# One memory plan for four chained stages: the first loads, roundings, norms and transposes of a stage are issued inside the stage before it

## The reference, cut to what matters

```python
x = x + tanh(g_xattn[0]) * _L0_xattn_ref(_layernorm(x), ctx, ctx, Wq, Wk, Wv, Wo, bo, g)
x = x + tanh(g_ffn[0])   * _L0_ffn_ref(_layernorm(x), Wb, bias, Wr, A, Bm)
x = x + tanh(g_xattn[1]) * _L1_xattn_ref(_layernorm(x), ctx, ctx, mask, Wq, Wk, Wv, Wo)
x = x + tanh(g_ffn[1])   * _L1_ffn_ref(_layernorm(x), weight, bias, gate_w, in_scale, out_scale)

# _L0_xattn_ref: linear attention, 8 heads of 64
qh = softmax(qh, axis=-2) * SCALE; kh = softmax(kh, axis=-1)
context = einsum('bhdn,bhen->bhde', kh, vh)
out = einsum('bhde,bhdn->bhen', context, qh)        # then Wo, bo and an L2 norm
# _L0_ffn_ref: x @ Wb.T + bias, plus a rank-16 mixture of 8 experts, top 2
# _L1_xattn_ref: 32 query heads on 8 key/value heads of 128, rotary positions
logits = 30 * tanh((q @ k.T) * 0.08838834764831845 / 30)
weights = softmax(where(mask, logits, -1e30)); out = (weights @ v) @ Wo
# _L1_ffn_ref: router softmax over 8, in_scale = routing @ in_channel_scale, ...
out = (xf * in_scale) @ sign(weight).T * out_scale + bias
```

## Time and profile before

| | |
|---|---|
| median of 3 runs | 3298.14 us (3297.99 to 3299.82) |
| profiled execution, its own time | 3307.61 us |
| span in the profile (first to last instruction) | 3305.8 us |
| PE busy | 3086.6 us (93%) |
| DVE, POOL, ACT busy | 2092.0, 1851.0, 1237.8 us |
| front stage ends, linear attention begins | 381.07 us |
| linear attention ends, attention begins | 1271.08 us |
| attention ends, FFN begins | 3056.57 us |

### The profile page before, as it was taken

One profiled execution on the slowest core, in us unless ns is written; L12 is line 12 of the kernel. 1 busy time (PEld: TensorE's weight loads), 2 busy tenths in 40 slices (PEclk: granted clock), 3 DMA queues, 4 the chain that ended last, 5 costly groups with the idle time before them and its releaser, 6 DMA issues. The chain is left out here.

```text
span 3305.8 us, 41113 instructions
## 1 busy us (share of the span) xinstructions
PE 3086.6 (93%) x14547; PEld 2478.6 (75%) x14547; DVE 2092.0 (63%) x2607; ACT 1237.8 (37%) x1898; POOL 1851.0 (56%) x1243
## 2 busy tenths in 40 slices
PE   7999679999999995899999999999999999998799
PEld 6888558788788774677777777777777787776677
DVE  3232257777777752667666767767776677675575
ACT  3111155555555531433333333433343434332322
POOL 4232255444454433666676767676767776664343
PEclk9999889999999997899999999999999999999699
DMA  7333501111101103222233222332223332321321
GB/s 199 110 126 112 176 26 39 65 45 52 64 33 65 52 32 132 94 101 102 89 127 140 102 95 95 121 146 95 95 95 109 121 138 91 118 100 53 143 71 51
DMA packets 171548, 315.66 MB, mean 95 GB/s; under 512 B 10360, under 2 KB 86776, under 8 KB 171432
## 3 DMA queue, kind: packets, MB, share of 16 engines
q1 hardware_dynamic: 171432, 314.17, 27.3%
HBM read 247.03 MB, written 67.11 MB: 95 GB/s over the span
## 5 line engine op out<-in xcount | busy, mean ns | idle before, releaser
L1783 DVE RECIPROCAL g_rsum<-gp_sum 128x512 f32<-128x512 f32 x128 | 429.1, 3352 | 58.1 <-PE gp_sum L1873 58.1
L1841 PE MATMUL gp_p<-g_xn_hi,g_wq_hi 128*128 128x512 f32 x1024 | 404.3, 395 | 28.5 <-POOL g_wq_lo L1529 28.5
L1841 PE MATMUL gp_p<-g_xn_lo,g_wq_hi 128*128 128x512 f32 x1024 | 403.3, 394 | 0.0
L1841 PE MATMUL gp_p<-g_xn_hi,g_wq_lo 128*128 128x512 f32 x1024 | 402.7, 393 | 0.0
L1897 PE MATMUL gp_y<-g_wo_hi,g_at_hi 128*128 128x512 f32 x992 | 389.4, 392 | 1.0
L1897 PE MATMUL gp_y<-g_wo_hi,g_at_lo 128*128 128x512 f32 x992 | 386.5, 390 | 0.0
L1897 PE MATMUL gp_y<-g_wo_lo,g_at_hi 128*128 128x512 f32 x992 | 386.5, 390 | 0.0
L1529 POOL TENSOR_TENSOR g_wq_lo<-g_wq_raw,g_wq_hi 128x1024 fp32r<-128x1024 f32 x130 | 310.4, 2410 | 1.6 <-ACT g_wq_hi L1627 1.6
L1529 POOL TENSOR_TENSOR g_at_lo<-g_at_raw,g_at_hi 128x512 fp32r<-128x512 f32 x128 | 179.8, 1404 | 217.1 <-ACT g_at_hi L1627 217.1
L1627 ACT ACTIVATE g_q_hi<-g_q_raw 128x512 fp32r<-128x512 f32 x128 | 81.2, 634 | 537.3 <-POOL g_q_raw L1560 537.3
L1744 DVE TENSOR_TENSOR g_q_raw<-gp_p,g_cos_q 128x512 f32<-128x512 f32 x128 | 88.6, 692 | 293.7 <-PE gp_p L1841 254.9
(11 more groups left out here) (255 smaller groups left out, 7341.5 us busy)
## 6 DMA issues: line engine op xcount, KB each, us to landing
g_wq_raw<-in_L_Wq SPq DMA_DIRECT2D x64, 1024.0 KB, 7.4
g_wo_raw<-in_L_Wo SPq DMA_DIRECT2D x62, 1024.0 KB, 6.4
values_split<-c_v SPq DMA_DIRECT2D x64, 256.0 KB, 2.8
keys_split<-c_k SPq DMA_DIRECT2D x32, 512.0 KB, 2.7
g_k<-keys_split SPq DMA_DIRECT2D x32, 512.0 KB, 3.3
g_v<-values_split SPq DMA_DIRECT2D x32, 512.0 KB, 7.7
c_cx_raw<-in_ctxT SPq DMA_DIRECT2D x16, 512.0 KB, 7.4
a_x<-in_x SPq DMA_DIRECT2D x16, 512.0 KB, 4.5
```

The source lines that it names most:

```text
L1783: V.reciprocal(rsum[:, :], p_sum[:, :]).then_inc(rsum_done, 1)
L1841: mm = M(bank[:, :], w[a][:, i, cols], x[b][:, i, :], start=(i == 0 and t == 0), stop=(i == KT - 1 and t == 2))
```

## The change

All tiles are placed by hand: `Arena` hands out fixed addresses from a start, and each stage lays its tiles out so that those which its successor fills early are over tiles that are already spent. The eight PSUM banks are allocated once and passed to all stages. A stage function now only builds its helpers and returns them, with a table `early` of pieces of work by engine; its `run` opens the block and calls the pieces of the next stage at fixed places of its own instruction streams. The blocks, and SP's waits for the last stores at their end, stay.

```diff
+class Arena:
+    def __call__(self, name, shape, dt=F32, over=None):
+        at = self.at if over is None else self.begins[over]
+        self.begins[name] = at
+        if over is None:
+            self.at = at + -(-4 * math.prod(shape[1:]) // 32) * 32
+        return self.nc.alloc_sbuf_tensor_at(self.prefix + name, shape, dt, offset=at)
...
 # front stage
-        rot = [sb(f"rot{i}", [P, BANK]) for i in range(2)]
+    rot = sb("rot", [P, BANK])
...
-                after(dve, rot_done, n - 2)
+        after(dve, rot_done, n - 1)
...
-            for dst, src in ((cos, cos_t), (sin, sin_t)):
+            for dst, src in ((cos, cos_t), (sin, sin_t), (m8, mask)):
...
+                    if j == NKV - 1 and g < 2:            # SP
+                        sp.wait_ge(made, made_k(j, g))
+                        early["sync"][g]()
                     store_k(j, g)
...
                     k_round(j, g)                         # ACT
+                    if j == NKV - 1 and g < 3:
+                        early["act"][g]()
...
+                if j < 3:                                 # DVE, between v_low and rotate
+                    (mask_rows, mask_turned, mask_tables)[j]()
+                if j == NKV - 1:
+                    early["dve"][0]()
                 for g in range(NGRP):
                     rotate(j, g)
+                    if j == NKV - 1 and g == 1:
+                        early["dve"][1]()
...
+                if j == NKV - 1:                          # POOL
+                    early["pool"][0]()
                 for g in range(NGRP):
                     finish_k(j, g)
+                    if j == NKV - 1 and 1 <= g < 3:
+                        early["pool"][g]()
...
+                if j == 1:                                # PE
+                    nc.tensor.transpose(p_m[:, 0:P], mf[:, :], ident[:, :]).then_inc(const_pe, 1)
+                if j == 2:
+                    M(p_m[:, 0:SEQ], ones[:, :], keep[:, :], start=True, stop=True).then_inc(const_pe, 1)
...
 # what linear attention gives the front stage
+    def first_loads():
+        load_x(0, early=True)
+        load_vo()
+        load_c(0, early=True)
+        load_ct(0, early=True)
+    def first_pool():
+        constants()
+        rstd_x(0, early=True)
+    def first_low():
+        wqk_low()
+        xn_lo(0, early=True)
+    early = {"sync": (first_loads, load_wqk),
+             "act": (lambda: c_hi(0, early=True), wqk_hi_parts, lambda: xn_hi(0, early=True)),
+             "dve": (first_moments, lambda: normal_x(0, early=True)),
+             "pool": (first_pool, lambda: c_lo(0, early=True), first_low)}
...
 # linear attention: where it runs the pieces of the attention stage
+                if s == BATCH:                            # SP
+                    sp.wait_ge(gathered, KT * BATCH)
+                    g.early["sync"][0]()                  # first_wq: 2 loads
+                step(s)
+                if s == BATCH:
+                    sp.wait_ge(qproj, KT * BATCH)
+                    sp.wait_ge(turned["q"], KT * BATCH)
+                    sp.wait_ge(out_done, 2 * BATCH)
+                    sp.wait_ge(n_store, 16 * 4)
+                    g.early["sync"][1]()                  # first_xn: 4 loads
...
                 add_bias(s - 2)                           # POOL
+                if s == BATCH + 1:
+                    g.early["pool"][1]()                  # xn_split(0, 0), wq_split(0, 1..3)
...
                 norm_scale(s - 1, 1)
+                if s == BATCH:
+                    g.early["pool"][0]()                  # wq_split(0, 0)
...
                 out_square(s - 1)                         # ACT
+                if s == BATCH:
+                    g.early["act"][0]()                   # wq to hi, 4 quarters
...
                 h_keep(s - 2)
+                if s == BATCH + 1:
+                    g.early["act"][1]()                   # xn to hi, 4 quarters
...
                 normal_x(s + 1)                           # DVE
+                if s == BATCH + 1:
+                    g.early["dve"][0]()                   # xn to lo, quarters 2 and 3
...
 # attention: the mask work and xn, wq loads are gone from its front
+            sp.dma_start(tg[:, :], gate).then_inc(const_in, 16)
             load_k(0)
             load_v(0)
...
+            steps(pool, body_pool)
+            pool.wait_ge(q_proj, FIRST + NGRP * NKV * NR)
+            f.early["pool"][0]()
...
+            steps(sp, body_sp)
+            f.early["sync"][0]()
...
+            steps(act, body_act)
+            f.early["act"][0]()
...
+            steps(dve, body_dve)
             for u in range(NU):
+                f.early["dve"][u]()
                 add_output(NGRP * NKV - 1, u)
+            f.early["dve"][NU]()
...
             for u in range(NU):                           # PE
                 output(last, u, wo_last)
+                if u == 1:
+                    pe.wait_ge(attn_done, FIRST + NGRP * NKV * NB)
+                f.early["pe"][u]()
...
 # what the FFN gives the attention stage
+    def first_loads():          # x 0, 1, gate table, gate, scale tables, 8 weight slices, x 2
+    def first_pool():           # constants, rstd 0 and 1, lo(0), lo(1)
+    def first_act():            # tanh, scale table to hi, signs, turn_out, exp, round_hi, scale_out
+    early = {"sync": (first_loads,), "pool": (first_pool,), "act": (first_act,),
+             "dve": (first_norms, first_applies, nothing, first_maxima, first_shares, first_scales, first_xs, nothing,
+                     nothing),
+             "pe": (nothing, first_turns, first_logits, nothing, first_routing, first_in_scales, first_out_scales, nothing)}
...
+        def _(_):               # FFN, SP: x 3 is the first load of its own block
+            load_x(3)
             sp.dma_start(tgb[:, :], bias).then_inc(bias_in, 16)
```

More of the change, by code:

```diff
@@ new lines, in k_count, with half, batch, bank @@
+    def k_count(j, g):
+        return j * NGRP + g + 1
+    def half(j):
+        return j * PER_J // BATCH
+    def batch(j, i):
+        return (j * PER_J + i) % BATCH
+    def bank(u):
+        return p_u[(u - 1) % NPS]
+    def after(engine, done, count):
+        if count > 0:
+            engine.wait_ge(done, count)
+    def tokens(b):
+        return lambda t: t[b // NB][:, :, (b % NB) * SEQ:(b % NB + 1) * SEQ]
+    def piece(i):
+        return lambda t: t[:, i * KT // PIECES:(i + 1) * KT // PIECES, :]
@@ new lines, in key_value_stage, with cx_ready, value @@
+    M = nc.tensor.matmul
+    def cx_ready(b):
+        if b < 8:
+            pe.wait_ge(cx_lo_dve, b + 1)
+        else:
+            pe.wait_ge(cx_lo_pool, b - 7)
+    def value(j, i):
+        u, q, b = made_v(j, i), half(j), batch(j, i)
+        after(pe, emptied, u - NPS)
+        if q == 0:
+            cx_ready(b)
+        for k in range(KT):
+            m, rest = divmod(k, KT // PIECES)
+            if b == 0 and rest == 0:
+                pe.wait_ge(wv_lo_dve if m % 2 else wv_lo_pool, PIECES // 2 * q + m // 2 + 1)
+            for t, (x, w) in enumerate(SPLIT):
+                mm = M(bank(u)[:, :], tokens(b)(cx[x])[:, k, :], wv[w][:, k, :],
+                       start=(k == 0 and t == 0), stop=(k == KT - 1 and t == 2))
+        mm.then_inc(made, 1)
@@ new lines, in key @@
+    def key(j, g):
+        u = made_k(j, g)
+        after(pe, emptied, u - NPS)
+        if g == 0:
+            pe.wait_ge(wk_lo, j + 1)
+        if j == 0:
+            for b in range(NB * g, NB * g + NB):
+                cx_ready(b)
+        for k in range(KT):
+            for t, (w, x) in enumerate(SPLIT):
+                mm = M(bank(u)[:, :], wk[w][:, k, :], cx[x][g][:, k, :],
+                       start=(k == 0 and t == 0), stop=(k == KT - 1 and t == 2))
+        mm.then_inc(made, 1)
@@ new lines, in linear_attention_moe_stage, with exists, after, steps @@
+    for u, unit in enumerate(in_turn):
+        bank_of[unit] = p_tr[u % 2]
+        if u >= 2:
+            kind, b, r = in_turn[u - 2]
+            bank_free[unit] = (kept[kind], b * UNITS_OF[kind] + r + 1)
+    def exists(b):
+        return 0 <= b < BATCH
+    def after(engine, done, count):
+        if count > 0:
+            engine.wait_ge(done, count)
+    def steps(step):
+        for s in range(-1, BATCH + 3 + 1):
+            step(s)
+    def heads(t):
+        return t.rearrange("p (h d) -> p h d", h=H)
@@ new lines, in attend, with out @@
+    def attend(n, first=False):
+        def out(u, heads_=range(G)):
+            if not first:
+                output(n - 1, u, wo, heads_)
+        out(0)
+        out(1)
+        scores(n, 0)
+        scores(n, 1)
+        out(2)
+        scores(n, 2)
+        values(n, 0)
+        out(3)
+        out(4, range(0, 2))
+        scores(n, 3)
+        values(n, 1)
+        out(4, range(2, G))
+        out(5)
+        out(6, range(0, 1))
+        values(n, 2)
+        out(6, range(1, G))
+        out(7)
+        values(n, 3)
@@ new lines, in main @@
```

(13 more changed lines are left out.)

3102 lines of the change are left out of this document (1523 added, 1579 removed).

## The result

The changed kernel takes 3283.93 us (median of 5 runs, 3279.89 to 3288.88) against 3299.82 us (5 runs, 3297.99 to 3300.35) for the kernel before on the same chip: ratio 0.9956, 95% interval 0.9942 to 0.9969, so by the ratio 14.5 us less (10 to 19). The forecast was 3273 with a range of 3250 to 3291. The direction and the places were right, the gain was 0.6 of what I had computed. The profiled execution took 3288.88 us, its span is 3287.1.

The account below looks back on a forecast made before the run. PE, busy 93% of the span, bounds the kernel, its idle time lying around three stage boundaries. Gains 3.8 + 12.6 + 9.7 - 0.8 = 25.3 us take the median from 3298.14 to 3273, range 3250 to 3291.

Parts of the forecast that it names:

- Barriers late, PE early: Stage boundaries: early work delays each barrier (6.7 us, then 7 and 17 less earlier shift), yet PE starts the next stage sooner.
- A: Boundary from front stage to linear attention: 3.8 us gained, PE's second stop still ending on x of batch 1.
- B: Boundary from linear attention to attention: 12.6 us gained, first projection at 1278.4 instead of 1291.06.
- From there on the stage runs as before: Linear attention after q_project(0, 5): the 3.8 us shift carries through unchanged.
- port rule: Linear attention to attention: DVE and POOL share an exclusive port pair; at worst POOL ends 2.4 us late, gain 11.2.
- C: Boundary from attention to FFN: 9.7 us gained, main product starting at 3091.9 instead of 3102.07.
- 8.2 at full: Attention to FFN: pair 0's prologue, 16.4 us of PE at half clock, takes 8.2 us at full clock.
- C gives nothing: Rival at attention to FFN: inserted pieces drop the clock, outputs 4 to 8 at half; gain -1, total 3283.5; chance 0.14.
- low bound for C: Attention to FFN: at least 3 us gained, with all outputs after the logits at half clock.
- Front stage: Front stage: small added PE, DMA and DVE work costs 0.8 us; the single rot buffer has 2.6 us to spare.
- the rival of the slower side: Front stage keys: POOL's add over 2.6 us later stalls the single rot buffer and PE; 3318 us, chance 0.06.
- It is wrong if a loop's pass changes its length: Stage loops: same work in the same order, so any changed pass length would refute the prediction; change claimed 0.

Follow-up runs that it names:

- A undone: Changed kernel with the early pieces of linear attention put back in that stage's own block: 3286.89 us, ratio 0.9956 to the kernel before.
- run 32: Not a follow-up run: "run" is a verb here, and the 32 small matmuls are pair 1's logits, 6.8 us at the lower clock level, 3.8 at the upper.
- the second experiment on B's tail: Changed kernel with POOL's wq then xn subtractions ahead of rstd_2(15), and DVE's xn quarters behind the last norm: 3277.79 us, ratio 0.9923 to the kernel before.

## Why the prediction was right in direction and too high

**Barriers late, PE early: right.** All three barriers moved later, by 5.8 (6.7 said), by 8.5 (7.0 less the shift so far) and by 11.2 us (24.2 with the 13.0 that had been gained by the 248th add, 17.2 said). In each the cause was the early work in front of the last store. In A and B the engine named, POOL, was the one: with its pieces elsewhere the barriers came at 382.97 and 1272.21.

**A, 3.8 said, 1.95 measured at the stop and 0.0 at `h_keep(0)`: mis-sized.** x of batch 1 ended the second stop as said, but it landed 21.8 us after the barrier and not 19.0 (408.69 less 386.90). I had taken the 17.0 us from the earlier trace rows, where the constants were already in the queue. From an empty queue the first four are tiny, and SP issues one each 0.47 us; the DMA line of the page, 0.65 us a figure from 386 to 412:

```profile
DMA  0001149899999999999999999999999930000000
GB/s 0 0 0 1 1 100 102 315 382 374 397 328 349 251 221 365 391 347 378 410 391 410 435 416 410 429 410 416 429 416 410 391 139 32 0 0 0 0 0 0
```

The flow is 100 GB/s from 2.4 us behind the barrier on, and above 300 only from 3.7. I had allowed about 2 us without a row for it. That left 1.95 us. "From there on the stage runs as before" failed too: from the sixth projection to `h_keep(0)` it takes 115.4 to 119.6 us, by the clock of the execution (A undone). One profile keeps its 2.1 us and the means keep nothing, so A is worth some 0 to 2 us at 530, and the profiles do not tell more.

**B, 12.6 said, 10.4 measured: the mechanism right, the tail too short.** POOL's five quarters took 13.6 us and not 13.0 and started 1 us later, since ACT's roundings stood behind `h_keep(15)`, itself 1.1 us late. The projection began 1.05 us behind the barrier and not 0.3. I had also missed that DVE's two quarters stand in front of the residual, which began at 1265.20, when `rstd_2(15)` had run at 1263.55 before; POOL, later still, hid that. The port rule of the Trainium skill (SBUF — State Buffer, "Who interferes with whom"), by which B would give 11.2, was the nearer in the number, but partly by luck: POOL's five took 1.6 us longer than the rows of before give (12.0), between the 1.0 that I had taken and the 2.4 of the rule's worst case, and the other terms of the miss are not the port's. My reading of the earlier trace rows, 1.22 us alone, was also too simple. Two of the eight (at 43.74 and 47.07) ran beside a POOL subtraction that had begun later, and it was POOL's that took 3.05 and 3.39 us instead of 2.4. The run with POOL's xn beside the norm shows the overlap on a single instruction: the same section of the Trainium skill lists `tensor_scalar` among the operations that can take the shared pair, and says that of two such instructions the one issued second waits the other out. The 2.75 us against 0.81 agree with it: the norm ended 0.56 us behind POOL's subtraction, which had begun 0.15 us ahead of it.

**C, 9.7 said, 5.6 measured: the price of the clock in the tail.** The stop on the scale tables (3.8 said, 4.18 measured) and the half-clock output behind it (2.7 said) were right: without them 7.2 us are gone. Wrong was "8.2 at full" for the prologue, and full clock for the outputs behind its pieces. The pieces took 12.3 us (2.2, 4.6, 0.4, 2.6 and 2.5, with 1.6 us of short waits in them), where I had 10.7 (8.2, and 2.5 for waits). The outputs cost more: the fourth began at the lower level behind the logits, the seventh and the eighth fell to it midway. They took 4.9, 4.3 and 4.2 us and not 2.7, together 5.3 us that the forecast had at nothing. PE's windows through the tail:

```profile
3030.00:3040.00 10.00, 10.00 (x37) 0.67 0.13 52
3040.00:3050.00 10.00, 5.82 (x15) 0.67 0.00 2
3050.00:3060.00 10.00, 8.53 (x28) 0.82 0.13 52
3060.00:3070.00 10.00, 3.52 (x10) 0.69 0.23 82
```

The rival "C gives nothing" had that mechanism; the measured value lies between it (-1) and the forecast. Its total, 3283.5, is within 0.5 us of the measured median, but by luck: it had A at 3.8 and B at 12.6. The forecast's low bound for C, 3, did not fit this rival either, which prices outputs 4 to 8 at 10.8 us more and so comes to -1. So the last add came 23.9 us late (10.8 later than before, though the 248th was 13.0 sooner), or 24.1 by the forecast's own count from the second of the last eight adds (3036.40 before, 3023.10 changed), and not 17.2. 3.1 us of that came back behind the barrier, where the logits of pair 1 ran at the upper clock level (`turn(2)` to `main` 9.3 us and not 12.4).

**Front stage, -0.8 said, 0 measured.** The 25th to 28th keys come within 0.1 us of before. The single `rot` buffer makes DVE wait for POOL's add twice before the last four keys (4.90 us at 62.17, 0.69 at 197.91), and PE has no stop between 50 and 372 us: the rival of the slower side was far off its point of decision.

**Not forecast.** The attention loop is 1.8 us shorter and linear attention's steps 0.4 us longer. Both are there in every profile of the new plan, the first within 1.2 us, the second within 0.03. "It is wrong if a loop's pass changes its length" was one of the prediction's own signs, and it came: here the statement that the loops do the same work in the same time failed, if only by 0.1%. The cause is open.

## What to carry to other kernels

Work that is pulled ahead of a barrier must be placed where its engine waits anyway, and behind every instruction of the chain to the last store: at B the order of three pieces on POOL and DVE was worth 7.4 us, on top of the 10.4 that the change had gained there. What is loaded first in a new block should be what ends the next stop (x of batch 1: 5.5 us shortly behind the stop, x of batch 3: 6), not what was written first. A piece slid between dense matmuls is to be priced at the lower clock level, and so are the dense ones behind it (at C 5.3 us, more than the pieces' own excess). A gain of 2 us at a stop is smaller than what the clock moves in the next 120 us, and one profile of each kernel does not show whether it arrives.

## What the runs showed of the hardware

- A DVE `tensor_scalar` of 128x1024 took 2.75 us instead of 0.81 when POOL had begun a subtraction 0.15 us before it, and POOL's 128x512 add 2.30 instead of 1.27 beside a DVE subtraction with two SBUF inputs that had begun 0.05 us before it.
- One execution can run 32 small matmuls in 6.8 us (6.83, lower clock level) and another of the same kernel in 3.9 (3.86, upper level); the two profiles of the kernel before differ by 4.7 us over boundary C alone.
- The same work from the sixth projection to `h_keep(0)` took 115.4, 117.1, 118.2 and 119.6 us in four profiles (A undone, the first of before, the changed kernel, the second experiment on B's tail); the granted clock from 470 to 490 us was 1.00, 1.00, 0.91 and 0.83 in them, and from 450 to 470 it was 1.00 in the first and 0.91 in the others.
- Two long stretches changed their length by about 0.1% (1600.0 to 1598.2 us, 694.44 to 694.85), alike in every profile of the new plan. Its tiles lie at other addresses; that this is the cause was not tested.
